# Layer norm taken apart: transposed x loaded, only the mean transposed, the spread applied to results

## The reference

```python
xn = (x - mean(x)) / sqrt(var(x) + 1e-5)          # no gain, no bias
# branch 1: linear attention, 16 heads of 32
Q = elu(xn @ wq.T + bq) + 1;  K = elu(xn @ wk.T + bk) + 1;  V = xn @ wv.T + bv
out = (Q @ (K.T @ V)) / (Q . sum(K) + 1e-8);  attn = out @ wo.T + bo
# branch 2: gated feed-forward, 1376 wide, shared and routed low-rank parts (top 2 of 8 experts)
scores = sigmoid(xn @ W_router);  w = top-2 weights of scores, normalised
gate = xn @ W_gate + lora(xn) + experts(xn, w);  up = xn @ W_up + lora(xn) + experts(xn, w)
hidden = silu(gate) * up
ffn = hidden @ W_down + lora(hidden) + experts(hidden, w)
x + attn + ffn
```

## Time and profile before

| | |
|---|---|
| median of 3 runs | 669.9 us (669.51 to 671.44) |
| profiled execution | 671.42 us, its span 669.6 us |
| PE busy | 659.4 us, 98% of the span, 3568 matmuls |
| PE loading weights | 545.9 us, 82% |
| DVE busy | 375.8 us, 56% |
| ACT busy | 257.5 us, 38% |
| POOL busy | 127.1 us, 19%, nearly all in the first 240 us |
| DMA | 74.21 MB, mean 111 GB/s |
| transposes of x (L1264) | 64 in 16 tiles |
| granted clock of PE | full but for the first 14 us |

### The profile page before, as it was taken

The page is one execution under the profiler, slowest core; times in us unless marked ns, Lnnn a source line. Parts: engine busy times, 40 slices in busy tenths (PEclk is TensorE's granted clock), DMA queues, the critical chain, the costliest instruction groups (busy, mean ns, idle before and its releaser), DMA issues.

```text
span 669.6 us, 10326 instructions
## 1 busy us (share of the span) xinstructions
PE 659.4 (98%) x3568; PEld 545.9 (82%) x3568; DVE 375.8 (56%) x698; ACT 257.5 (38%) x413; POOL 127.1 (19%) x290
## 2 busy tenths in 40 slices
PE   6999999999999999999999999999999999999998
PEld 5998999977777788888888888888888888888886
DVE  5677888778775956334345443445444326534433
ACT  4444454467235423323233333243233324323321
POOL 3466566626246230000000000000000000000000
PEclk8999999999999999999999999999999999999999
DMA  7875666644754679940025100011400001300001
GB/s 222 300 258 192 209 224 220 231 181 141 288 218 158 238 217 3 45 160 0 1 78 200 52 0 0 0 67 76 187 0 0 0 5 73 126 0 0 0 0 63
DMA packets 41642, 74.21 MB, mean 111 GB/s; under 512 B 19392, under 2 KB 20288, under 8 KB 39952
## 3 DMA queue, kind: packets, MB, share of 16 engines
q1 hardware_dynamic: 38672, 64.52, 34.6%
q10 hardware_dynamic: 2736, 9.05, 3.5%
q0 software_dynamic: 208, 0.30, 0.2%
HBM read 52.81 MB, written 21.04 MB: 110 GB/s over the span
## 4 chain that ended last, share of the span: by engine, by line
PE 94%; DVE 3%; DMA 1%; ACT 1%; issue 0%; SPq 0%; DVEq 0%
PE bank L1245 21%; PE bank L1246 21%; PE bank L1247 21%; PE bank L1490 18%; PE bank L1463 6%; DVE den L1091 2%; PE bank L1474 1%; PE bank L1476 1%; PE bank L1264 1%; DMA xin<-in_x 1%; PE bank L1276 1%; PE bank L1363 1%; PE bank L1501 1%; PE bank L1503 1%; PE bank L1285 0%
## 5 line engine op out<-in xcount | busy, mean ns | idle before, releaser
L1245 PE MATMUL bank<-x,up_h 128*128 128x512 f32 (+1 forms) x352 | 137.1, 390 | 0.2 <-DVE x3r L1056 0.2
L1247 PE MATMUL bank<-x,up_l 128*128 128x512 f32 (+1 forms) x352 | 137.0, 389 | 0.0
L1246 PE MATMUL bank<-x,up_h 128*128 128x512 f32 (+1 forms) x352 | 137.0, 389 | 0.0
L1182 DVE TENSOR_TENSOR hf<-bank,silu 128x512 f32<-128x512 f32 x44 | 30.4, 691 | 155.0 <-issue 135.3
L1490 PE MATMUL bank<-dn,hid_h 128*128 128x512 f32 x352 | 108.7, 390 | 0.0
L677 ACT ACTIVATE hid_h<-hf 128x512 fp32r<-128x512 f32 x44 | 27.8, 632 | 144.0 <-DVE hf L1182 144.0
L1245 PEld LDWEIGHTS bank<-x,up_h 128*128 128x128 f32 x352 | 66.1, 188 | 14.5 <-issue 0.7
L1490 PEld LDWEIGHTS bank<-dn,hid_h 128*128 128x128 f32 x352 | 65.9, 188 | 14.4 <-DVE res L1207 0.6
L1247 PEld LDWEIGHTS bank<-x,up_l 128*128 128x128 f32 x352 | 66.1, 188 | 13.8
L1246 PEld LDWEIGHTS bank<-x,up_h 128*128 128x128 f32 x352 | 66.1, 188 | 13.7
L888 DVE TENSOR_TENSOR up_l<-up_raw,up_h 128x1024 fp32r<-128x1024 f32 x44 | 54.9, 1249 | 28.1 <-ACT up_h L677 28.1
(11 more groups left out here) (166 smaller groups left out, 1083.4 us busy)
## 6 DMA issues: line engine op xcount, KB each, us to landing
x<-scr_x SPq DMA_DIRECT2D x7, 2048.0 KB, 8.5
up_raw<-in_ffn_up SPq DMA_DIRECT2D x11, 768.0 KB, 7.6
scr_x<-xt ACTq DMA_DIRECT2D x16, 512.0 KB, 4.5
xin<-in_x SPq DMA_DIRECT2D x16, 256.0 KB, 4.3
scr_z<-zt SPq DMA_DIRECT2D x16, 256.0 KB, 2.2
x3r<-in_x SPq DMA_DIRECT2D x16, 256.0 KB, 3.4
scr_att<-x3r SPq DMA_DIRECT2D x16, 256.0 KB, 2.8
z<-scr_z SPq DMA_DIRECT2D x4, 1024.0 KB, 4.8
```

The costliest lines, as they stand in the source:

```text
L1182: nc.vector.tensor_tensor(hf[:], ps_u[:], silu[:], ALU.mult).then_inc(h_done, 1)
L1245: nc.tensor.matmul(dst, lh, rh, start=start, stop=False, **kw)
L1246: nc.tensor.matmul(dst, lh, rl, start=False, stop=False, **kw)
L1247: return nc.tensor.matmul(dst, ll, rh, start=False, stop=stop, **kw)
```

## The change

Layer norm is not applied to x any more. The host hands in x a second time, transposed (xT), and each tile of it is loaded into a new buffer xtr. PE transposes only the mean, spread over 128 columns, in one operation behind V-z (mean_rows), and DVE subtracts it from the transposed tile (centre). Everything behind works on these deviations, and the inverse spread is applied to results: K in the operation that adds its bias, V in ACT's copy, the router's logits in the exp, the queries by a new product on DVE with a row of inverse spreads (query_scaled), the gate by a new product on DVE ahead of silu (gate_scaled), and the outcome of the down product in the operation that adds it to res. For the rows, POOL keeps each tile's inverse spread, SP stores it in DRAM (scr_r) and loads it broadcast to all partitions, 512 tokens at a time. Tiles 0 and 1 are still transposed by PE from x less its mean. POOL's rstd_of has four operations instead of two and is called one tile later. At the start the load of tile 1 goes behind two loads of wk, and DVE's statistics of tile 1 go behind the first remainder of wv. ps_q and ps_g are freed by the new products.

```diff
             load_x(0, 0)
             sp.dma_start(ident[:], dram["ident"]).then_inc(ident_in, 16)
-            load_x(1, 1)
             for k in range(1, KD, 2):
                 sp.dma_start(w_raw[:, 0, k], dram["wkT"][:, k]).then_inc(wk_in[k], 16)
+            load_x(1, 1)
...
+            def load_xt(t, s):
+                wait(sp, xtl_done, t - 1)
+                sp.dma_start(xtr[:, s:s + 1].rearrange("p o k n -> p o (k n)"),
+                             dram["xT"][:, bass.ds(t, 1)].rearrange("p o k n -> p o (k n)")).then_inc(xtr_in[s], 16)
...
             def stage1(t, s, more=True):
                 if more:
 
-                    sp.wait_ge(ln_done, t + 2)
+                    sp.wait_ge(ln_done if isinstance(t, int) and t == 0 else ln_stats, t + 2)
                     load_x(t + 3, 1 - s)
-
+                    load_xt(t + 3, 1 - s)
+                if ahead(t, 1):
+                    store_rstd(t + 1)
...
-            def rstd_of(t):
+            def rstd_of(t, s):
 
                 pool.wait_ge(ln_stats, t + 1)
-                nc.gpsimd.tensor_tensor(vare[:], mv[:, 1:2], epsln[:], ALU.add).then_inc(vare_done, 1)
+                nc.gpsimd.tensor_tensor(vare[:], mv[:, s, 1:2], epsln[:], ALU.add).then_inc(vare_done, 1)
                 pool.wait_ge(vare_done, t + 2)
-                nc.gpsimd.tensor_tensor(rstd[:], vare[:], mhalf[:], ALU.pow).then_inc(ln_rstd, 1)
+                nc.gpsimd.tensor_tensor(rs[:, s:s + 1], vare[:], mhalf[:], ALU.pow).then_inc(rs_done, 1)
+                pool.wait_ge(rs_done, t + 1)
+                nc.gpsimd.tensor_tensor(nrs[:, s:s + 1], rs[:, s:s + 1], minus[:], ALU.mult).then_inc(ln_rstd, 1)
+                nc.gpsimd.tensor_tensor(rstd[:, bass.ds(t, 1)], rs[:, s:s + 1], one[:], ALU.mult).then_inc(rstd_done, 1)
...
                 if more:
-                    rstd_of(t + 3)
+                    rstd_of(t + 2, s)
...
             def query_relus(g, c):
                 n = g * KD + c
-                act.wait_ge(q_ready, n + 1)
+                act.wait_ge(qs_done, n + 1)
                 wait(act, q_done, n - 1)
-                nc.scalar.activation(qexp[:, c % 2, :], ps_q[c % 2][:], ACT.Relu, scale=-1.0,
-                                     bias=nbq[:, c:c + 1]).then_inc(qrelu_done, 1)
-                nc.scalar.activation(qf[g % 2][:, c, :], ps_q[c % 2][:], ACT.Relu, bias=bq_c[:, c:c + 1]
-                                     ).then_inc(qmax_done, 1)
+                q = qf[g % 2][:, c, :]
+                nc.scalar.activation(qexp[:, c % 2, :], q, ACT.Relu, scale=-1.0, bias=nbq[:, c:c + 1]).then_inc(qrelu_done, 1)
+                nc.scalar.activation(q, q, ACT.Relu, bias=bq_c[:, c:c + 1]).then_inc(qmax_done, 1)
...
-                act.wait_ge(g_ready, n + 1)
-                nc.scalar.activation(silu[:], ps_g[:], ACT.Silu).then_inc(silu_done, 1)
+                act.wait_ge(gs_done, n + 1)
+                nc.scalar.activation(silu[:], silu[:], ACT.Silu).then_inc(silu_done, 1)
...
+            def centre(t, s, uses):
+                dve.wait_ge(xt_ready, t + 1)
+                dve.wait_ge(xtr_in[s], 16 * uses)
+                nc.vector.tensor_tensor(xtr[:, s], xtr[:, s], ps_xt[:, s * P:(s + 1) * P].unsqueeze(1).to_broadcast([P, KD, P]),
+                                        ALU.subtract).then_inc(ln_done, 1)
...
             def tokens_lo(t, s):
+                early = isinstance(t, int) and t < 2
                 dve.wait_ge(xth_done, t + 1)
-                sub(xt_l[:, s].rearrange("p k n -> p (k n)"), ps_xt[:], xt_h[:, s].rearrange("p k n -> p (k n)")
-                    ).then_inc(xtl_done, 1)
+                src = ps_xt[:].rearrange("p (k n) -> p k n", n=P) if early else xtr[:, s]
+                sub(xt_l[:, s], src, xt_h[:, s]).then_inc(xtl_done, 1)
...
-                if ahead(t, 2):
-                    normalise(t + 2, s)
                 dve.wait_ge(vz_ready, t + 1)
                 if behind(t, 2):
                     dve.wait_ge(zst_done, t - 1)
                 nc.vector.tensor_copy(zraw[:, s], ps_z).then_inc(zraw_done, 1)
+                if ahead(t, 2):
+                    centre(t + 2, s, half + 1)
...
+            def query_scaled(g, c):
+                dve.wait_ge(q_ready, g * KD + c + 1)
+                dve.wait_ge(rb_in[g % 2], 16 * (g // 2 + 1))
+                if g > 1:
+                    dve.wait_ge(qnl_done, (g - 1) * KD)
+                nc.vector.tensor_tensor(qf[g % 2][:, c, :], ps_q[c % 2][:], rb[g % 2][:], ALU.mult).then_inc(qs_done, 1)
...
-            queries(0, (0,))
+            for par in range(2):
+                dve.wait_ge(scr_xd[par], 16 * TILES // 2)
+            query_scaled(0, 0)
             key_values(TILES - 1, TILES // 2 - 1)
             heads_of(1)
-            queries(0, (1,))
+            queries(0, (0,))
+            query_scaled(0, 1)
             lora_weighted(TILES - 1, (TILES - 1) % 2)
             lora_lo(TILES - 2)
-            queries(0, (2,))
+            queries(0, (1,))
+            query_scaled(0, 2)
             dve.wait_ge(bdnh_done, 1)
             sub(bdn[0:ER, 1], bdn_raw[0:ER, 1], bdn[0:ER, 1]).then_inc(bdn_done, 1)
+            queries(0, (2,))
+            query_scaled(0, 3)
             queries(0, (3,))
             m_lo(0, (0, 1))
             reciprocals(0)
+            query_scaled(1, 0)
             m_lo(0, (2, 3))
             dve.wait_ge(bdn_done, 1)
             reciprocal_lo(0)
+            queries(1, (0,))
+            query_scaled(1, 1)
             scaled(0, (0, 1))
-            queries(1, (0,))
+            queries(1, (1,))
             scaled(0, (2, 3))
-            queries(1, (1,))
+            query_scaled(1, 2)
             kvt_lo(1)
             lora_lo(TILES - 1)
             queries(1, (2,))
+            query_scaled(1, 3)
             m_lo(1, range(KD))
             queries(1, (3,))
             group(1)
...
                 if not last and not start:
                     split_up(c + 1, 1 - s, n + 2)
-                split_dn(c, s, n + 1)
                 if due is not None:
                     due()
+                gate_scaled(n, g)
+                split_dn(c, s, n + 1)
...
-                        nc.vector.tensor_tensor(res[:, j, :], res[:, j, :], ps_out[j][:], ALU.add).then_inc(o_done, 1)
+                        nc.vector.scalar_tensor_tensor(res[:, j, :], ps_out[j][:], r, res[:, j, :], ALU.mult, ALU.add).then_inc(o_done, 1)
...
+            def mean_rows(t, s):
+                pe.wait_ge(ln_stats, t + 1)
+                pe.wait_ge(xtl_done, 2)
+                wait(pe, ln_done, t - 1)
+                nc.tensor.transpose(ps_xt[:, s * P:(s + 1) * P], mv[:, s, 0:1].to_broadcast([P, P]), ident[:]
+                                    ).then_inc(xt_ready, 1)
...
-                if ahead(t, 1) and not first:
-                    transpose_tokens(t + 1)
...
+                if ahead(t, 2):
+                    mean_rows(t + 2, s)
                 if behind(t, 2):
                     lora_transposed(t - 2)
...
-                    wait(pe, qmax_done, g * KD + c - 1)
+                    wait(pe, qs_done, g * KD + c - 1)
...
-                dst, free, ready = ((ps_g, silu_done, g_ready), (ps_u, h_done, u_ready))[a]
+                dst, free, ready, uses = ((ps_g, gs_done, g_ready, n), (ps_u, h_done, u_ready, n + 1))[a]
```

More of the change, by code:

```diff
@@ L70, with program @@
 }
-def program(nc, dram, out, scr_x, scr_z, scr_att, scr_w):
+def program(nc, dram, out, scr_x, scr_z, scr_att, scr_w, scr_r):
     ctx = ExitStack()
@@ L84, in program @@
         wtok = sb("wtok", [P, E, TILES])
+        rstd = sb("rstd", [P, TILES])
         bdn = sb("bdn", [P, 2, D], F32R)
@@ L127, in program @@
         kvt_l = at("kvt_l", [P, KD, P], F32R)
+        rb = [rb_even, at("rb_odd", [P, GN])]
+        assert place[0] <= wq_at + 4 * UPC
         place[0] = wq_at + 4 * UPC
@@ L602, in links, with route @@
                 return link
-            def route(t, more=True):
+            def route(t, s, more=True):
                 link = links(t)
@@ L638, in _ @@
             pool.dma_start(zmask[:], dram["zmask"]).then_inc(consts_in, 16)
-            rstd_of(2)
-            with pool.Fori(0, TILES - 3) as t:
-                route(t)
-            route(TILES - 3, more=False)
+            with pool.Fori(0, TILES // 2 - 1) as p:
+                route(2 * p, 0)
+                route(2 * p + 1, 1)
             def key_sums(b):
@@ L959, in stage1 @@
                 wait(dve, kf_done, t)
-                nc.vector.tensor_tensor(kb[:], ps_k[:], bk_b[:], ALU.add).then_inc(kb_done, 1)
+                dve.wait_ge(ln_rstd, t + 1)
+                nc.vector.scalar_tensor_tensor(kb[:], ps_k[:], rs[:, s:s + 1], bk_b[:], ALU.mult, ALU.add).then_inc(kb_done, 1)
                 if not first:
@@ L1126, in group @@
                 if not last:
+                    query_scaled(g + 1, 0)
+                scaled(g, (3,))
+                if not last:
                     queries(g + 1, (0,))
```

(14 more changed lines are left out.)

116 lines of the change are left out of this document (83 added, 33 removed).

## The result

The changed kernel took **737.6 us** (median of six runs, 733.3 to 739.3) against 669.6 us before it on the same chip: a ratio of 1.100, 95% interval 1.097 to 1.103, so 68 us slower. The forecast was 684.3 us with a range of 674 to 691. The sign was right; 50 of the 68 us come from a step that the forecast had called small.

What follows compares the result with a forecast made beforehand. PE nearly full, but POOL's loop to set stage 1's pace and DVE and ACT turns stage 2's: +2.1, +3.95, +1.8, +3.45, +0.85, +0.6, +1.65 = +14.4 on the median 669.9, 684.3 us; range 674 to 691.

Steps and rivals of the forecast that it cites:

- extra DMA: Transposed x (3.7 MB) and row loads cost nothing; the 16 stores of rstd and their loads are small.
- What the differences were taken from: Whole kernel: +14.4 us against the profiled execution (671.4 us), then added to the median of 669.9 us.
- Start: Start of stage 1: bk_b's load comes late, K of tile 1 starts at 21.25 us, +2.4 (bounds +0.8 and +3.4).
- Stage 1 turns on POOL: Routing loop: eq +0.33 us, 7.7 us a tile where wq or wo is split, 7.27 elsewhere; stage 1 ends +2.1.
- rival (b): Stage 1: no contention on eq (ends 2.6 us earlier), or bk_b in time: 681.7 us, both about 680; chance 0.22.
- Four queries of group 0: Stage 2, group 0: new DVE products make each turn 3.2 us; denominators(0) +3.95 us, PE idles about 4.7 us.
- Clock: Stage 2, after PE's idle: slow clock makes denominators(0) take 1.9 us instead of 1.07, +0.85 (bounds 0 and 3.5).
- To expand(0), to denominators(1): Stage 2: denominators(0) to expand(0) 9.2 us, +1.8; expand(0) to denominators(1) 19.3 us, +3.45.
- Stage 2 in all: All stage 2 terms: +3.95, +1.8, +3.45, clock +0.85 and later groups +0.6, 10.65 us in all.
- Rival (a): PE decides after all: matmuls of group 0 and m hide the DVE and ACT turns, 669.3 us; chance 0.13.
- Stage 3: Gate products for 44 chunks: hidden behind the up product, except that the second gate starts late, +1.65 us.

Runs made afterwards that it cites:

- e3: Kernel before plus 16 stores of one 128 x 1 column, one per tile, 4-byte elements as neighbours in DRAM: 723.7 us.
- e4: Kernel before plus the 14 loads of transposed x (256 KB each) into a buffer that nobody reads: 669.6 us.
- e6: Kernel before plus 16 stores of 128 separate 4-byte elements, each element 512 bytes from the next: 669.25 us.
- e7: Kernel before plus 16 stores at the same places as in e3, each of 128 whole rows of 512 bytes: 669.6 us.
- e9: e8 with the load of bk_b issued on POOL's queue ahead of the spread of tile 1, not behind it: 683.7 us.
- e8: Changed kernel, complete, without column stores: rstd transposed once by PE and stored as 16 rows of 512 bytes: 687.6 us.
- e13: e8 with the edits of e9, e10, e11 and e12 all together: 669.4 us.
- e12: e8 with the remainder of x taken, from tile 2 on, with one SBUF source in place of two (values wrong): 686.4 us.
- e10: e8 without the DVE query products of stage 2; ACT reads the unscaled queries straight from PSUM: 677.1 us.
- e11: e8 without the 44 DVE gate products of stage 3; silu reads the unscaled gate straight from PSUM: 687.3 us.

## Why the prediction was wrong, and where it was right

**The step that failed** is the sentence on extra DMA: "The 16 stores of rstd and their loads are small". They are small, 512 bytes each, and cost 49.5 us. The forecast weighed DMA by its bytes and by the lead that each transfer has. It gave the store's form no bounds, though the trace of before shows no store of a column of 4-byte neighbours in stage 1, and an unseen form is just what should be bounded from both sides. One row of the kernel before would have warned, the only store by elements that it has:

```profile
scr_w<-wtok SPq DMA_DIRECT2D x1, 64.0 KB, 36.7
```

64 KB in 36.7 us, at a place where PE had no wait for it. The table of stretches of the same trace has the sign of e3 in it while this store is under way, a share over 1 with next to nothing moved (whether other transfers were due is not shown):

```profile
255.00:262.00 7.00, 7.00 (x33) 5.79 (x32) 3.50 (x6) 2.02 (x3) 0.00 (x0) 1.00 1.92 2
```

The second half of the failure is who waits: the stores hold back other transfers for some 5 us, and ACT, in order, waits for every z store before it may write zt.

**The rest of the sum** can be read in e1, the changed kernel without these stores: 688.2 us, 3.9 above the forecast and inside the range. Its three marks, columns as in the earlier trace rows:

```profile
154.03 1.94 PE L1472 MATMUL bank<-qf_even,kcur 128*32 128x512 f32 x8 [4.34 <-DVE qf_even L1125]
164.97 0.51 PE L1481 MATMUL bank<-rr,hrow 32*128 32x512 f32 x4 [1.23 <-DVE rr L1172]
184.94 1.07 PE L1472 MATMUL bank<-qf_odd,kcur 128*32 128x512 f32 x8
```

- **What the differences were taken from.** The forecast took them from the profiled execution of the kernel before (671.4 us), with its stretch at half the clock from 10.3 to 13.8 us, and added them to the median (669.9). e4, e6 and e7 are the kernel before with additions that cost nothing; their profiled executions took 669.3 to 669.8 us and have no such stretch, and K of tile 1 starts at 16.84, 16.68 and 17.22 us, against 18.86. e1 has none either. So the terms for the start and for stage 1 are some 2.4 us too small.
- **Start.** K of tile 1 was to start at 21.25 us and starts at 21.70 in e1. As a time that is right, as a price not: +5.0 us against e6, forecast +2.4. Stage 1 was to pass on 2.1 us to the first DVE product of a query, at 138.85; it starts at 139.04, again right as a time, and +4.5 against e6, whose sum in that place starts at 134.55. The bound for a load that is in time, +0.8, was near: e9 starts K of tile 1 at 17.86 us, +1.2 against e6, and its first query product at 129.34, with e6's 129.15. So without the late load stage 1 ends where it did before. Part of the price of the late load can be clock, which the forecast left out here. In e8's trace PE idles 3.40 us, and the matmuls behind take 0.63 us each, at a granted clock of 0.70 from 20 to 30 us, a mix of its two levels (1.2 and 2.4 GHz); in e9's they take 0.40; in e1's PE idled 1.25 us in that row and kept its clock:

```profile
19.98 0.47 PE L1374 MATMUL bank<-ident_sb,mv 128*128 128x128 f32 x1 [3.40 <-DVE mv L956]
...
21.11 0.63 PE L1350 MATMUL bank<-wk_h,xt 128*128 128x512 f32 x1
```

- **Stage 1 turns on POOL.** Right. eq went from 0.33 us to 0.70 in 13 of 16 tiles (e9); from tile 8 to 10 the loop takes 7.70 us a tile in e9 (eq at 81.11 and 96.51), forecast 7.7, and PE waits 0.76 and 0.75 us for the statistics ahead of the mean transposes at 98.40 and 113.78 us. From tile 2 to 7 the loop takes 7.35; the 7.27 of the forecast is its sum without the longer eq, and gives no reason for leaving it out there, where it is 0.70 too. In e13, with eq at 0.44, it is 7.45 (80.45 and 95.34), where the transposes had set 7.54 before. The Trainium skill, SBUF — State Buffer, "Who interferes with whom", had this right: two SBUF inputs contend. e12 meant to take the contention away and only shortened it: its one-source form runs 0.42 us, and eq 0.43, ending 0.17 us behind it. The Trainium skill has that in the same section: such a form can enter a mode that takes the shared ports; the prediction told the rule without this exception. So e12 is no clean zero, and rival (b)'s 2.6 us stay untested.
- **Four queries of group 0.** denominators(0) was to come at 150.95 + 2.1 = 153.05 and came at 154.03. The idle of PE in front was to be 4.7 us and was 4.34. Right, and the turn too: 3.28 us, forecast 3.2.
- **Clock.** Forecast 1.9 us for denominators(0) after the idle; 1.94, at a granted clock of 0.50. Right.
- **To expand(0), to denominators(1).** Forecast 10.05 us with the slow clock, and 19.3; found 10.94 and 19.97 in e1. The excess is clock. e8 takes 10.06 and 18.38: there matmuls are back at 0.39 us from 159.15 us, 3.3 us behind the start of denominators(0), in e1 the clock stood at 0.50 up to 160, 6 us behind. And in the second stretch, after the same idle of 2.39 us, the clock was 0.70 in e1 and 1.00 in e8:

```profile
179.32:184.94 5.62, 5.62 (x21) 3.67 (x21) 3.62 (x6) 0.00 (x0) 0.00 (x0) 0.70 0.99 364
...
180.26:184.28 4.02, 4.02 (x20) 2.49 (x20) 3.64 (x6) 0.00 (x0) 0.02 (x1) 1.00 0.93 326
```

  The pieces that the forecast lists for the second stretch add up to 20.3 us and not to 19.3; both are above the 18.38 of a full clock.
- **Stage 2 in all** was tested by e10: 10.5 us, forecast 10.65. Rival (a), that the matmuls hide these turns, falls.
- **Stage 3.** The second gate waits 1.6 us for its product, forecast 1.65; what it is worth at the end (0.3 us in e11) is below what can be told. The other 43 products are hidden, as forecast.

So of e1's distance to the forecast, 5.1 us when its span is held against e6's (19.5 against 14.4), 2.4 are from the start and stage 1, 0.8, 0.9 and 0.7 from the three marks of stage 2, and 0.3 from behind them. e1 lies in the range, but by the width of the range: the largest part of its distance has a cause that the forecast did not name.

## What to carry to other kernels

Before a store is called small, ask how its elements lie in memory: here a column out of SBUF into a contiguous row of DRAM sent 128 pieces to one place and held up the transfers of the core. Turn it into a row first (one small transpose for many columns), or space the elements. A stall of PE is priced with the clock behind it, not by its length alone. And look at the granted clock of the trace from which a forecast takes its rows: a stretch at the low clock that the median doesn't have is part of the difference.

## What the runs showed of the hardware

- Behind a store of 128 elements of 4 bytes to 512 neighbouring bytes the DMA of the core moved 23 and 42 GB/s for 5.5 us in two places of e3, where it moves 231 on average without them; 16 such stores cost 49.5 and 54 us. The same elements 512 bytes apart, and 128 rows of 512 bytes, cost nothing that can be measured (669.25 and 669.6 against 669.4 us).
- 2048 such elements in one store took 12.4 us with the core's DMA nearly still; the same 8 KB as 16 rows landed in 1.4 us by the list of DMA issues.
- 14 loads of 256 KB added to a stage that already moved 231 GB/s cost nothing that can be measured (669.6 us).
- After 3.4 us and 4.3 us of idle PE ran at the lower of its two clocks (matmuls of 0.63 us for 0.39; the group of eight 1.94 for 1.06, granted clock 0.50); after 1.2 us it did not. After 2.4 us at the same instructions it did in e1 and e9 (0.70 and 0.69) and did not in e8 (1.00).
- The kernel before came with and without a stretch at 0.51 of the clock near 10 us; it puts all later marks 2.2 us back (e6 against the earlier trace rows).
